# A two-layer recurrent kernel: the input products of layer one by seven block products, the two weight parts of layer two side by side in PSUM

## What is computed

```python
def lstm_step(carry, xw_t):                 # layer 0: xW = x @ Wx0 + b0, Wx0 512 x 2048
    a = xw_t + prev_h @ Wh                  # Wh 512 x 2048
    i, f, o = sigmoid(a[:, :H]), sigmoid(a[:, H:2*H]), sigmoid(a[:, 2*H:3*H])
    next_c = f * prev_c + i * tanh(a[:, 3*H:])
    next_h = o * tanh(next_c)
x = x + lstm(x, cond, Wx0, Wh0, b0)
def rnn_step(h, xw_t):                      # layer 1: xW = x @ Wx1 + b1, both weights 512 x 512
    h_next = tanh(h @ Wh + xw_t)
x = x + rnn(x, cond, Wx1, Wh1, b1)
```

## Time and profile before

| | us |
|---|---|
| median of 3 runs | 2285.53 (2284.49 to 2286.43) |
| the profiled execution | 2284.95 |
| its span, first to last instruction | 2283.1 |
| mean granted TensorE clock, share of full | 0.993 |

### The profile page before, as it was taken

One profiled execution on the slowest core, in us unless ns is written; L12 is line 12 of the kernel. 1 busy time (PEld: TensorE's weight loads), 2 busy tenths in 40 slices (PEclk: granted clock), 3 DMA queues, 4 the chain that ended last, 5 costly groups with the idle time before them and its releaser, 6 DMA issues.

```text
span 2283.1 us, 150617 instructions
## 1 busy us (share of the span) xinstructions
PE 2242.1 (98%) x65564; PEld 1617.7 (71%) x65564; DVE 1976.7 (87%) x10283; ACT 1644.5 (72%) x5662; POOL 1.8 (0%) x10
## 2 busy tenths in 40 slices
PE   5999999999999999999999999999999999999997
PEld 2777777777777777777777777777777777777775
DVE  6888888888888888888888888888888888888887
ACT  5777777777777777777777777777777777777775
POOL 0000000000000000000000000000000000000000
PEclk7999999999999999999999999999999999999999
DMA  5000000000000000000000000000000000000000
GB/s 210 18 13 18 23 23 18 14 18 23 23 18 23 13 18 23 23 18 13 18 23 23 18 23 13 18 23 23 18 13 22 19 23 18 23 14 18 23 13 13
DMA packets 16738, 54.03 MB, mean 24 GB/s; under 512 B 2256, under 2 KB 2384, under 8 KB 14800
## 3 DMA queue, kind: packets, MB, share of 16 engines
q1 hardware_dynamic: 16080, 44.41, 5.5%
HBM read 27.62 MB, written 16.78 MB: 19 GB/s over the span
## 4 chain that ended last, share of the span: by engine, by line
PE 97%; DVE 1%; ACT 1%; DMA 1%; issue 0%; SPq 0%; POOL 0%; DVEq 0%; ACTq 0%
PE rec_ps L178 39%; PE in_ps L178 38%; PE rnn_ps L178 20%; DMA wh_sb<-wh 1%; ACT wh_part L480 0%; DVE wh_part L318 0%; DVE largest_slice L277 0%; DVE turned L350 0%; DVE uv L362 0%; DVE h_parts L378 0%; DVE pre_sb L356 0%; ACT wx_sb L468 0%; DVE turned L400 0%; ACT gates_cell L504 0%; ACT rnn_ps L500 0%
## 5 line engine op out<-in xcount | busy, mean ns | idle before, releaser
L178 PE MATMUL in_ps<-wx_sb,x_sb 128*32 128x512 f32 x8192 | 976.4, 594 | 18.4 <-ACT wx_sb L468 18.4
L178 PE MATMUL rec_ps<-wh_part,h_parts 128*32 128x256 f16 x32704 | 988.9, 273 | 5.3 <-DVE h_parts L386 5.3
L178 PEld LDWEIGHTS rec_ps<-wh_part,h_parts 128*32 128x32 f16 x32704 | 867.4, 97 | 13.1 <-issue 8.0
L350 DVE STREAM_TRANSPOSE turned<-rec_ps 128x256 f32<-128x256 f32 x1024 | 461.0, 450 | 196.7 <-PE rec_ps L178 151.5
L178 PEld LDWEIGHTS in_ps<-wx_sb,x_sb 128*32 128x32 f32 x8192 | 259.0, 110 | 327.7 <-issue 319.1
L178 PEld LDWEIGHTS rnn_ps<-wx_sb,y 128*32 128x32 f32 x8192 | 247.0, 110 | 302.5 <-issue 301.0
L490 ACT ACTIVATE rec_ps<-in_ps,mask_scaled 128x256 f32<-128x256 f32 x1022 | 406.6, 435 | 0.4 <-issue 0.2
L178 PE MATMUL rnn_ps<-wh_part,h_parts 128*32 128x128 f16 x16352 | 323.9, 219 | 7.9 <-DVE h_parts L414 7.9
L178 PE MATMUL rnn_ps<-wx_sb,y 128*32 128x128 f32 x8192 | 318.5, 273 | 1.3 <-ACT rnn_ps L500 1.3
L504 ACT ACTIVATE gates_cell<-gate_ps,unscale 128x128 f32<-128x128 f32 x511 | 187.9, 368 | 180.7 <-DVE gate_ps L356 180.7
L500 ACT ACTIVATE rnn_ps<-rnn_ps,mask_scaled 128x128 f32<-128x128 f32 x511 | 174.8, 342 | 188.7 <-DVE turned L400 188.5
(11 more groups left out here) (52 smaller groups left out, 1276.0 us busy)
## 6 DMA issues: line engine op xcount, KB each, us to landing
x_sb<-xT SPq DMA_DIRECT2D x32, 512.0 KB, 3.8
yT<-y SPq DMA_DIRECT2D x64, 256.0 KB, 2.0
wh_sb<-wh SPq DMA_DIRECT2D x5, 1024.0 KB, 9.7
wx_sb<-wx SPq DMA_DIRECT2D x5, 1024.0 KB, 14.4
b_sb<-b SPq DMA_DIRECT2D x1, 256.0 KB, 2.7
b_sb<-b SPq DMA_DIRECT2D x1, 64.0 KB, 12.2
h_first<-h0T SPq DMA_DIRECT2D x1, 32.0 KB, 11.6
```

What stands on the lines that cost most here:

```text
L178: last = nc.tensor.matmul(out[QUAD * q:QUAD * (q + 1)], states, weights(q), start=False, stop=True, tile_position=(0, QUAD * q), skip_grou ...
L350: nc.vector.transpose(turned0[:, half].rearrange("p b n -> p (b n)"), rec0_ps[t % 2][half][:, 0:COLSH]).then_inc(turned0_done[half], 1)
```

## The change

- **Seven products.** For a span of four steps, x (two pairs of steps) and Wx0 are each seen as two by two blocks, and the four blocks of the result come from seven block products of sums of blocks instead of eight. The sums of Wx0's blocks are made once by GpSimd (`sum_wx0`, four sums of 2048 elements per partition), those of x by GpSimd in four iterations of every sixteen (`sum_x`, 256 elements each). A product is two units of four fp32 products of 256 columns; the 14 units of a span are dealt to four iterations as 4, 3, 4, 3 (`units`). Three more copies or additions of 256 columns join the blocks: `copy_v` and `begin_c11` on ScalarE where t mod 4 is 0, `begin_c12` on VectorE where it is 1, `finish_c22` on VectorE where it is 2. The bias copies become `bias_z` (t mod 4 is 3) and `bias_v` (2), 256 columns each.
- **Layer 1's recurrence.** The high and low parts of Wh1 stand side by side, so `recurrent1` is 16 products of 256 columns that leave two partial sums. ScalarE copies one of them to SBUF (`copy_low1`), VectorE adds the other (`sum1`), and `turn1` turns the sum from SBUF. `seed1` writes 256 columns instead of 128.
- **Order.** On VectorE `sum1`, the extra addition and `turn1` now stand ahead of `turn0(0)`, `add1` between `turn0(0)` and `add0(0)`; `state_high(0)` stands ahead of `cell(1)`; `add_y1` stands between the full value and the low part of half 1. On ScalarE `seed0` is one instruction for each half at its own place, and half 1 has one PSUM bank instead of two. Wh1's scale and parts are made in iterations 2 and 3. `input1` is dealt as 3 and 1 slices.

The diff, cut to its core:

```diff
+UNITS_OF_PART = (0, 4, 7, 11, 14)
+SLOTS = SPAN * SPANS - 5
...
+            def reduce_largest(l):
                 pool.wait_ge(largest_done, l + 1)
                 nc.gpsimd.partition_all_reduce(largest_all[l][:, :], largest[l][:, :], P,
                                                bass.bass_isa.ReduceOp.max).then_inc(reduced, 1)
+            def sum_x(v, i):
+                x = x_sb[:, v % 2].rearrange("p k (g r t) n -> p r k g (t n)", g=PER_CHUNK, r=2)
+                a11, a12, a21, a22 = x[:, 0, 0:SUBH], x[:, 0, SUBH:SUB], x[:, 1, 0:SUBH], x[:, 1, SUBH:SUB]
+                sums = x_sums[:, v % 2]
+                if i == 0:
+                    pool.wait_ge(x_in[v % 2], loads(v))
+                    if v >= 2:
+                        pool.wait_ge(slot_done, slots_until((v - 1) * CHUNK - 6))
+                if i in (1, 3):
+                    pool.wait_ge(x_summed, 4 * v + i)
+                out, one, op, other = ((sums[:, 0], a21, ALU.add, a22), (sums[:, 1], sums[:, 0], ALU.subtract, a11),
+                                       (sums[:, 2], a11, ALU.subtract, a21), (sums[:, 3], a12, ALU.subtract, sums[:, 1]))[i]
+                nc.gpsimd.tensor_tensor(out, one, other, op).then_inc(x_summed, 1)
+            def sum_wx0(i):
+                b11, b12 = wx0_sb[:, 0:SUBH, :, 0:COLSH], wx0_sb[:, 0:SUBH, :, COLSH:COLS]
+                b21, b22 = wx0_sb[:, SUBH:SUB, :, 0:COLSH], wx0_sb[:, SUBH:SUB, :, COLSH:COLS]
+                if i < 2:
+                    pool.wait_ge(wx0_doubled, SUBH * (i + 1))
+                if i in (1, 3):
+                    pool.wait_ge(wx0_summed, i)
+                one, other = ((b12, b11), (b22, wx0_sums[:, 0]), (b22, b12), (b21, wx0_sums[:, 1]))[i]
+                nc.gpsimd.tensor_tensor(wx0_sums[:, i], one, other, ALU.subtract).then_inc(wx0_summed, 1)
+            pool.wait_ge(b0_doubled, 1)
+            nc.gpsimd.tensor_tensor(b0_diff[:, :], b0_sb[:, COLSH:COLS], b0_sb[:, 0:COLSH], ALU.subtract).then_inc(b0_diff_done, 1)
+            for i in range(4):
+                sum_x(0, i)
+            reduce_largest(0)
+            for i in range(4):
+                sum_wx0(i)
+            reduce_largest(1)
+            for t in range(STEPS):
+                v, c = divmod(t, CHUNK)
+                if 3 <= c < 7 and v + 1 < CHUNKS:
+                    pool.wait_ge(rec0_done[0], t + 1)
+                    sum_x(v + 1, c - 3)
...
+            def units(g, first, end):
+                z = z_ps[g % 2]
+                products = (
+                    (z, lambda k: x_pair(g, 0, k), wx0_block(0, 0)),
+                    (v_ps[g % 2], lambda k: x_sum(g, 0, k), wx0_sum(0)),
+                    (z, lambda k: x_sum(g, 1, k), wx0_sum(1)),
+                    (c11_ps, lambda k: x_pair(g, 0, SUBH + k), wx0_block(1, 0)),
+                    (z, lambda k: x_sum(g, 2, k), wx0_sum(2)),
+                    (c12_ps, lambda k: x_sum(g, 3, k), wx0_block(1, 1)),
+                    (z, lambda k: x_pair(g, 1, SUBH + k), wx0_sum(3)),
+                )
+                sum_of = {1: 0, 2: 1, 4: 2, 5: 3}
+                for u in range(first, end):
+                    j, k = divmod(u, 2)
+                    if k == 0:
+                        if j == 0 and g % PER_CHUNK == 0:
+                            pe.wait_ge(x_in[g // PER_CHUNK % 2], loads(g // PER_CHUNK))
+                        if j in sum_of:
+                            sums_ready(g, sum_of[j])
+                    out, states, weights = products[j]
+                    last = tiles(out, states(k), lambda q: weights(k, q))
+                last.then_inc(slot_done, 1)
...
-                    for part in weights:
-                        last = tiles(rec1_ps, states[:, k], lambda q: part[:, k, q])
+                    if s:
+                        last = tiles(rec1_ps, h1_parts[:, k], lambda q: wh1_parts[:, k, q].rearrange("p b w c -> p (b w c)"))
+                    else:
...
-                    p, half = divmod(t + 3, PAIR)
-                    if p < PAIRS:
-                        input0(p, half)
+                    recurrent0(t)
+                    if t < SLOTS:
+                        g, part = divmod(t + 5, SPAN)
+                        pe.wait_ge(seed0_done[0], t + 2)
+                        if part == 0:
+                            pe.wait_ge(z_biased, g - 1)
+                        elif part == 1:
+                            pe.wait_ge(c11_begun, g)
+                        elif part == 2:
+                            pe.wait_ge(c12_begun, g)
+                        else:
+                            pe.wait_ge(c22_done, g)
+                            if g + 1 < SPANS:
+                                pe.wait_ge(v_biased, g)
+                        units(g, UNITS_OF_PART[part], UNITS_OF_PART[part + 1])
                 s = t - LAG
...
+            def begin_c12(g, t):
+                dve.wait_ge(slot_done, slots_until(t - 1))
+                dve.wait_ge(v_copied, g)
+                dve.wait_ge(seed0_done[1], t + 1)
+                nc.vector.tensor_tensor(c12_ps, z_ps[g % 2], v_sb[:, :], ALU.add).then_inc(c12_begun, 1)
+            def finish_c22(g, t):
+                dve.wait_ge(slot_done, slots_until(t - 1))
+                if g >= 2:
+                    dve.wait_ge(seed0_done[1], SPAN * (g - 1))
+                nc.vector.tensor_tensor(c22_sb[g % 2][:, :], z_ps[g % 2], v_sb[:, :], ALU.add).then_inc(c22_done, 1)
...
+            def sum1(s):
+                dve.wait_ge(rec1_copied, s + 1)
+                nc.vector.tensor_tensor(rec1_sum[:, :, :], rec1_by_part[:, :, 0], rec1_low[:, :, :],
+                                        ALU.add).then_inc(rec1_summed, 1)
             def turn1(s):
-                dve.wait_ge(rec1_done, s + 1)
-                nc.vector.transpose(turned1[:, :].rearrange("p b n -> p (b n)"), rec1_ps).then_inc(turned1_done, 1)
+                dve.wait_ge(rec1_summed, s + 1)
+                nc.vector.transpose(turned1[:, :].rearrange("p b n -> p (b n)"),
+                                    rec1_sum[:, :].rearrange("p b c -> p (b c)")).then_inc(turned1_done, 1)
...
             for t in range(END):
...
+                n, s = t + 1, t - LAG - 1
+                lstm, rnn = t < STEPS, s >= 0
+                g, part = divmod(t + 5, SPAN)
+                if t == 0:
+                    rnn_largest()
+                    dve.wait_ge(cell_zeroed, 1)
+                if rnn:
+                    sum1(s)
+                if lstm and t < SLOTS:
+                    if part == 2:
+                        begin_c12(g, t)
+                    elif part == 3:
+                        finish_c22(g, t)
                 if rnn:
                     turn1(s)
                 if lstm:
...
+                    turn0(0, t)
                 if rnn:
                     add1(s)
...
+                if lstm:
+                    add0(0, n)
+                    turn0(1, t)
+                    add0(1, n)
+                    gate_products(0, n)
+                if rnn:
+                    state1_high(s)
+                if lstm:
+                    cell(0, n)
+                if rnn:
+                    state1_low(s)
+                if lstm:
+                    gate_products(1, n)
+                    state_high(0, n)
+                    cell(1, n)
+                    state_full(0, n)
+                    state_low(0, n)
+                    state_high(1, n)
+                    state_full(1, n)
+                if rnn:
+                    add_y1(s)
+                if lstm:
+                    state_low(1, n)
+                    add_y0(t)
...
+            def copy_v(g):
+                if g >= 2:
+                    act.wait_ge(c22_done, g - 1)
+                nc.scalar.activation(v_sb[:, :], v_ps[g % 2], ACT.Copy).then_inc(v_copied, 1)
+            def begin_c11(g):
+                return nc.scalar.activation(c11_ps, z_ps[g % 2], ACT.Copy)
...
+            def seed0(half, t):
+                g, part = divmod(t, SPAN)
+                source = ((c11_ps, c12_ps) if part < PAIR else (z_ps[g % 2], c22_sb[g % 2][:, :]))[half]
+                if half == 0 and t >= 2:
+                    act.wait_ge(turned0_done[0], t - 1)
+                if half == 1 and t >= 1:
+                    act.wait_ge(turned0_done[1], t)
                 own = (mask_scaled[0] if t else mask)[:, t % PAIR:t % PAIR + 1]
-                for half in range(HALVES):
-                    last = nc.scalar.activation(rec0_ps[t % 2][half][:, 0:COLSH], in0_ps[t // PAIR % 2][:, half * COLSH:(half + 1) * COLSH],
-                                                ACT.Copy, scale=own)
-                last.then_inc(seed0_done, 1)
+                return nc.scalar.activation(rec0_ps(t, half), source, ACT.Copy, scale=own).then_inc(seed0_done[half], 1)
...
+            def copy_low1(s):
+                act.wait_ge(rec1_done, s + 1)
```

(44 more changed lines are left out.)

211 lines of the change are left out of this document (119 added, 92 removed).

## The result

| us | before | after |
|---|---|---|
| median (lowest to highest, 20 runs each) | 2285.72 (2284.14 to 2288.26) | 2280.58 (2276.04 to 2289.59) |
| the profiled execution | 2284.95 | 2289.59 |
| its span | 2283.1 | 2287.8 |

After stands to before as 0.9979 (95% interval 0.9972 to 0.9985): 5 us faster, where 30 were forecast. The profiled execution of after is the slowest of its twenty, 9 us above their median.

A forecast was written before the change was run, and what follows sets the result against it. TensorE was taken to bound the kernel at 4.345 us per iteration, then layer 0's cycle at a mean of 4.25. Against 2284.95, -48 for 503 iterations, +15 start and +3 end gave 2255 us, range 2207 to 2293.

The forecast's parts named there:

- the likeliest case: Layer 0's cycle limits the loop to a mean of 4.25 us; 2235 to 2273 us with the start's bounds, chance 0.50.
- the wait that the forecast counted on: TensorE idle ahead of slice 2 of half 0, released by half 1's low part.
- The step that failed: ScalarE: ScalarE some 84% busy, not the bound; `c11` reaches TensorE 0.1 late where t mod 4 is 0, costing nothing by itself.
- The cycle by half 1: Layer 0, from slice 2's products to the next: 1.55 plus 2.67, with 0.14 for handing over, is 4.22 us.
- a start every 4.14, not binding: Layer 0's half 0: low part at X+1.83 instead of 1.95 would allow a recurrence start every 4.14 us.
- The rival that TensorE stays the bound: Hand-over much quicker than seen, so iterations take 4.11 to 4.18; 2205 us at 4.15; chance 0.14.
- TensorE's iteration, 4.11: TensorE's work per iteration: 1.75 recurrence, 1.93 input products of both layers, 0.435 layer 1's recurrence; 0.23 less than before.
- The extra addition ahead of the turn: VectorE's addition of 0.35 to 0.38 ahead of `turn0(0)` makes X 0.13 late; counted in one of four iterations.
- The exclusive port: Rival: GpSimd's SBUF reads exclude VectorE's two-input instructions; 12 us for 124 sums, 5 to 8 at the start; 2274, chance 0.16.
- The start, 15 us: GpSimd's late reduction and four Wx0 sums of 4.2 us delay iteration 3's turn to about 66; bounds 9 to 32.
- The end, 3 us: Four last iterations of layer 1 alone each get the copy and `sum1` in series, 0.70 each.
- the prediction's own marks: Distance 4.25, wrong under 4.18 or over 4.31, if `turn0(0)` always waits for the copy, or GpSimd lengthens VectorE's two-input instructions.

The follow-up runs named there:

- experiment 1: Changed kernel with ScalarE's `bias1` moved back ahead of `gates(0)`, nothing else: 2225.17 us, 0.9733 of the kernel before.
- experiment 4: Kernel before the change with only `bias1` moved behind `tanh_cell(0)`: 2363.91 us, 1.0342 of the kernel before.
- experiment 11: Changed kernel, sums of x released by `add_y0`, another start, layer 0's input products on 64 of 256 columns, `bias1` left behind `tanh_cell(0)`: 2250.73 us, 0.9842.
- experiment 9: Changed kernel, `bias1` early, sums of x released by `add_y0`, another start, layer 0's input products cut to 64 of 256 columns: 2198.41 us, 0.9621.
- experiment 10: Kernel before the change with layer 0's input products cut to 128 of 512 columns: 2246.49 us, 0.9832.
- experiment 6: Changed kernel with `bias1` early and GpSimd's real sums of x released by the end of the previous iteration's `add_y0`: 2213.04 us, 0.9684.
- experiment 2: Changed kernel without GpSimd's 124 sums of x inside the loop: 2274.70 us, 0.9954 of the kernel before.
- experiment 5: Changed kernel with `bias1` early and GpSimd's 124 sums of x in the loop replaced by fills: 2212.64 us, 0.9680.
- the version with the new start: Changed kernel, `bias1` early, GpSimd's reduction ahead of the sums of x, sums of Wx0 on VectorE, two Wx0 doublings ahead of the scale wait: 2211.35 us, 0.9676.

## Why the prediction was wrong

It gave 2255 with a range of 2207 to 2293. The time, 2280.6, lies in the range, but the step behind the likeliest case did not hold, and the gain was a sixth of the 30 us forecast. That it lies in the range is luck: the wait that the forecast counted on, at slice 2 by half 1, did not come, and the largest one that came was not in its sum. By the table above the loop gave back 22 us and not 48, with the start 22 and not 15.

- **The step that failed: ScalarE.** The prediction added up ScalarE's work and looked at one wait behind it, that of `c11`. It did not follow `bias1`, which the diff shows moving behind `tanh_cell(0)`, to the one that waits for it, TensorE's `input1`. The trace of before had it: half 0's tanh is the first row below, the next instruction on ScalarE starts at 1005.34, and a copy of 0.27 put there ends at 1005.61, behind the start of `input1` at 1005.51. The missed term is 0.087 per iteration, 44 us, and with the single long iterations 55 (experiments 1, 4 and 11). ScalarE's share of the span, put at 84%, is 78%; it says nothing on this wait.

```profile
1005.20 0.20 ACT L514 ACTIVATE gate_ps<-gates_cell 128x32 f32<-128x32 f32 x1
1005.34 0.21 ACT L509 ACTIVATE o_scaled<-gates_cell 128x32 f32<-128x32 f32 x1
```

- **The cycle by half 1: mis-sized.** The prediction had half 1 done at X+2.53, and that is what the bare cycle shows (X = 1003.28 - 4.146 + 1.98 = 1001.11; done 1003.65). The 0.14 for handing over, read at a recurrence's start, was put on slice 2 in its middle too, where it is at most 0.07. So half 1 does not bind at 4.22. Half 0's "a start every 4.14, not binding" is the true bound, at 4.146 (experiment 9). For the old order it said 4.26 by half 0, measured 4.254 (experiment 10). The rival that TensorE stays the bound named the right length (4.11 to 4.18) and the right doubt, the hand-over.
- **TensorE's iteration, 4.11.** 4.13 by the starts of its groups; it does not show itself in the time, since the cycle stands 0.02 over it.
- **The extra addition ahead of the turn, 0.13 in one of four iterations.** It did not come. The iterations with and without `c12` or `c22` have the same median. From the copy's start to half 0's turn, with the extra addition between, 1.18 was taken and about 1.1 is measured (the copy lasts 0.28, not 0.34), and X is still released by TensorE, at R+1.98.
- **The exclusive port.** Its price in the loop was 12 us for 124 sums, 0.1 each, and is 12 (experiment 6). Its price at the start was put at 5 to 8; it is larger, below.
- **The start, 15 us.** It is 22. The reduction came at 26.27 (28.2 forecast): a change of GpSimd's work does cost, 8.28 and 8.70, but what the 10.25 ahead of the iota was the earlier trace rows is not shown, since the iota now starts at 1.77 with 0.29 of idle time, and in experiments 2 and 5 has 10.1 and 10.0 ahead of it again. The sums of Wx0 took 4.8 each (4.2 was chosen, between 2.1 and 8.4) and ended at 54.84 (55 forecast). What failed is the consequence drawn: iteration 2 was to wait for them, but VectorE's splitting stood beside them and four of its instructions became as long as a whole GpSimd sum, so already iteration 1 started late, 16.05 us of idle TensorE. By the row of all fourteen executions in that stretch (shortest, median, longest):

```profile
L452 DVE SCALAR_TENSOR_TENSOR wh_part<-wh_sb,w_scale,wh_part x14: 739/749/5049, 30.1 to 56.6; 128x512 f16<-128x512 f32 x14
```

- **The end, 3 us.** It is 4.

By the prediction's own marks: iteration 3's turn "at about 66" came at 73.7; the distance, 4.309, is at the edge of the "4.31" from which it called itself wrong; TensorE is not held ahead of slice 2; and VectorE's two-input instructions are longer beside GpSimd's, the last of its marks.

## What to carry to other kernels

Follow each moved instruction to its reader, also one that is cheap and on an engine at 78%: in a cycle of engines the time at which it ends counts, and an average of busy time says nothing on that. A group of matmuls that starts 0.1 behind another engine's end in every second iteration is a wait, even where the page shows no idle time for it; the median distance of iterations, taken by their place in the pattern, finds it. Idle time without a releaser should be set against the landings of the engine's instruction packets before it is called unexplained. A hand-over measured at one point should be measured again, or bounded to zero, before it is put on another.

## What was not expected of the hardware

- A VectorE instruction of 0.75 us took 5.0 beside GpSimd's sum of 4.8 us, and one of 0.18 took 0.48 beside a sum of 0.73. A sum of 2048 elements took 4.70 to 4.97 on GpSimd and 2.28 on VectorE. The Trainium skill (GPSIMD Engine Reference, section 3.1) has 4497 and 2293 ns for an addition of that size; the trace agrees on VectorE, and GpSimd's were some 5 to 10% longer here, beside VectorE's work. GpSimd is held up too: the sums of x that take 0.73 alone take 1.06 to 1.19 beside VectorE's splitting in the version with the new start.
- Behind a reduction over partitions, or ahead of one, GpSimd stood idle for 7.4 to 11.8 us, over all runs, when the kind of its work changed and no releaser shows. It is no fixed price: ahead of the second reduction of after the whole gap, with a wait for VectorE in it, was 6.0.
- From the end of the instruction waited for to TensorE's next product it took 0.14 behind VectorE's low part, 0.10 behind ScalarE's bias, 0.21 behind VectorE's cell, and at most 0.07 at slice 2 within a recurrence.
- Stopping TensorE in every second iteration ahead of layer 1's input brought further single delays of 0.2 to 1.4 us elsewhere, in six kernels with such a stop, 14 to 32 us in all; in those without one it was 3 to 10. They stand where a new block of 256 instructions begins, and the first instruction of a block never started less than 1.17 us behind a landed packet in after. What makes the packets late is open.
